# Part of the source-row look-ups of a graph attention stage moved from GpSimd gathers to TensorE one-hot products

## The reference, cut to what matters

```python
h = (x_flat @ W_gat).reshape(M, HEADS, NUM_EXPERTS)          # M = 32768 nodes, 4 heads x 4 values
a_src = (h * att_src).sum(-1);  a_dst = (h * att_dst).sum(-1)
e = leaky_relu(a_src[src] + a_dst[dst], negative_slope=0.2)   # one value per edge and head
e_max = segment_max(e, dst);  ee = exp(e - e_max[dst])
denom = segment_sum(ee, dst); alpha = ee / (denom[dst] + 1e-16)
agg = segment_sum(h[src] * alpha[:, :, None], dst) + b_gat    # 16 values per node
...                                                           # top 2 of 4 gates per node
for ei in range(NUM_EXPERTS):
    hh = gelu(x @ W1[ei] + b1[ei]);  out = out + g[..., None] * (hh @ W2[ei] + b2[ei])
```

## Time and profile before

| | us |
|---|---|
| median of three runs | 10518.87 |
| profiled execution, its own time | 10541.24 |
| span of that execution | 10539.5 |
| `edge_states`, its first DMA issue to the end of its last scan | 4594.0 to 9925.8 |
| busy in the span: GpSimd / TensorE / Vector / Scalar | 5766.4 / 4945.6 / 4253.4 / 2154.3 |

### The profile page before, as it was taken

One profiled execution on the slowest core, in us unless ns is written; L12 is line 12 of the kernel. 1 busy time (PEld: TensorE's weight loads), 2 busy tenths in 40 slices (PEclk: granted clock), 3 DMA queues, 4 the chain that ended last, 5 costly groups with the idle time before them and its releaser, 6 DMA issues. The chain is left out here.

```text
span 10539.5 us, 77438 instructions
## 1 busy us (share of the span) xinstructions
PE 4945.6 (47%) x21339; PEld 2904.5 (28%) x21339; DVE 4253.4 (40%) x9137; ACT 2154.3 (20%) x4043; POOL 5766.4 (55%) x5263
## 2 busy tenths in 40 slices
PE   6888888689936888821112111122111122111145
PEld 5556555567722444410000000000000000000011
DVE  5665665556679878711111111111111111111178
ACT  3434344333311222211111111111111111111000
POOL 2333333300032455367777777777777777777662
PEclk9888898899968999965556555556555556555577
DMA  2000000021110222131111111111111111111455
GB/s 89 34 34 26 26 25 24 38 77 57 57 58 30 54 55 52 34 71 33 34 36 36 38 33 34 33 37 39 33 34 33 34 36 39 34 33 34 59 183 187
DMA packets 388197, 510.48 MB, mean 48 GB/s; under 512 B 216517, under 2 KB 303358, under 8 KB 365442
## 3 DMA queue, kind: packets, MB, share of 16 engines
q1 hardware_dynamic: 191618, 258.32, 8.6%
q0 software_dynamic: 163968, 75.75, 6.3%
q10 hardware_dynamic: 32256, 171.98, 4.1%
HBM read 245.58 MB, written 263.86 MB: 48 GB/s over the span
## 5 line engine op out<-in xcount | busy, mean ns | idle before, releaser
L1663 POOL DMA_INDIRECT e_row<-rows_dram,e_idx x4096 | 4058.6, 991 | 1263.2 <-issue 1247.2
L1609 PE MATMUL e_bank<-e_hid,e_w 128*128 128x512 f32 x1024 | 591.7, 713 | 4217.1 <-ACT e_hid L1639 4217.1
L1696 DVE COPY e_idx<-e_allidx 128x64 int32 x64 | 13.8, 215 | 4374.0 <-DMA e_row<-rows_dram,e_idx 4374.0
L1609 PEld LDWEIGHTS e_bank<-e_hid,e_w 128*128 128x128 f32 x1024 | 220.7, 223 | 4520.3 <-issue 4520.3
L1647 ACT ACTIVATE e_ex<-e_dx 128x512 f32<-128x512 f32 x64 | 40.3, 630 | 3605.3 <-DVEq L1709 3605.3
L387 POOL COPY a_xc<-a_xp 128x1573 f32<-128x1573 f32 x104 | 405.9, 3907 | 678.1 <-PE a_bank L441 563.7
L1047 POOL DMA_INDIRECT c_yt<-yb_dram,keep_slots x256 | 383.0, 1496 | 587.0 <-DVE c_yg L1267 507.7
L396 POOL DMA_INDIRECT xb_dram<-a_so,a_sidx x256 | 251.6, 983 | 739.7 <-DVE a_sidx L669 490.5
L1602 PE MATMUL e_bank<-e_h,e_w 128*128 128x512 f32 x1024 | 508.4, 626 | 77.6 <-DMA e_h<-hn_dram 77.6
L199 DVE TENSOR_TENSOR a_cnta_hot<-a_cnta_iota,a_cnta_part 128x512 bf16<-128x512 bf16 x1184 | 519.9, 439 | 0.0
L1168 PE MATMUL c_conv<-c_xp,c_w 128*128 128x512 f32 x1152 | 513.7, 600 | 0.0
(11 more groups left out here) (352 smaller groups left out, 10083.1 us busy)
## 6 DMA issues: line engine op xcount, KB each, us to landing
e_row<-rows_dram,e_idx POOLq DMA_INDIRECT x4096
ys_dram<-e_y ACTq DMA_DIRECT2D x64, 1024.0 KB, 3.9
f_ye<-ys_dram SPq DMA_DIRECT2D x64, 1024.0 KB, 4.8
res_dram<-e_st ACTq DMA_DIRECT2D x64, 768.0 KB, 3.3
xb_dram<-a_taps SPq DMA_DIRECT2D x4, 5120.0 KB, 31.1
b_tok<-xb_dram SPq DMA_DIRECT2D x80, 256.0 KB, 2.7
yb_dram<-b_y ACTq DMA_DIRECT2D x80, 256.0 KB, 2.0
x_dram<-a_xs SPq DMA_DIRECT2D x9, 2048.0 KB, 6.3
```

The lines of the kernel that those rows point to most:

```text
L1609: mm = nc.tensor.matmul(bank[UPB + n % DNB][:], w2[:, n % NE, f], hid[:, n % 2, f], start=(f == 0), stop=(f == NF1 - 1))
L1663: nc.gpsimd.indirect_dma_start(row[:, s, u], None, rows, bass.IndirectOffsetOnAxis(ap=idx[:, s, u:u + 1], axis=0)).then_inc(gath[s], 16)
```

## The change

- Of the 64 edges of a chunk and partition, GpSimd now gathers the rows of 50 (`UP`). The last 14 (`XG`) are looked up on chip.
- The node table is loaded once into SBUF as `table` by 8 DMAs of 4096 pieces of 64 bytes each: node = (s, g, l), with l (0 to 127) the partition, g (8) and s (32). Only the 16 values of `h` are in it.
- `code` holds the low 10 bits of the source index, `high` the upper 5. For look-up k TensorE spreads the 128 codes over all partitions (L1629, a product with the identity, into PSUM `spread`), Vector compares them with the 8 x 128 low numbers and so makes the one-hot weights `hot` (L1772, 1024 elements), TensorE multiplies them with the table in 8 products of 128x128 by 128x512 (L1642, into PSUM `found`), and Vector masks the 32 candidates by the upper bits (L1791, 512 elements) and sums them (L1796, 512 to 16). `found`, `hot` and `prod` have two buffers each. After 14 look-ups Vector works out `a_src` of these edges (L1799 to L1801).
- TensorE's list is now, for each chunk: look-ups 0 and 1, the expert step, look-ups 2 to 13. The one-hot weights of look-ups 0 and 1 of the next chunk are made in this one.
- Vector does the 14 look-ups of a chunk ahead of all its former work on it.
- Scalar runs one expert step before the loop, and then the step of chunk n + 1 ahead of the exponentials of chunk n.
- The exponentials go to PSUM (`ex`), those used as weights also to SBUF (`weight`) by a second activation. The banks left for the experts are two for `up` and two for `down`.
- The wait for the stored states at the end of each turn is now a wait of each chunk for its own buffer. Scalar clears the semaphores of the block `experts` in `partition_starts`.

The core of the diff (declarations and the passing of arguments are left out):

```diff
         @block.sync
         def _(sp):
-            sp.dma_start(allidx[:, 0:FE], srcs).then_inc(consts, 16)
+            sp.dma_start(allidx[:, 0:FE], srcs).then_inc(listed, 16)
+            for g in range(HG):
+                sp.dma_start(table[:, g], table_g[g][:, :, 0:HF]).then_inc(tabled, 16)
             for dst, src in ((w1[:], w["w1"].rearrange("e d f -> d e f")),
                              (w2[:], w["w2"].rearrange("e (f p) d -> p e f d", p=P)),
-                             (b1[:], w["b1"]), (b2[:], w["b2"])):
+                             (b1[:], w["b1"]), (b2[:], w["b2"]), (att[:], att_src.broadcast_to([P, HF]))):
                 sp.dma_start(dst, src).then_inc(consts, 16)
 
...
         @block.tensor
         def _(pe):
+
+            def spread_code(k):
+                s, j = divmod(k % (2 * XG), XG)
+                nc.tensor.matmul(spread[:], code[:, s, j:j + 1].broadcast_to([P, P]), ident[:], start=True,
+                                 stop=True).then_inc(code_spread, 1)
+
             pe.wait_ge(consts, 80)
+            pe.wait_ge(coded, 1)
+            spread_code(0)
+            pe.wait_ge(tabled, 16 * HG)
             with pe.Fori(0, TURNS) as i:
+                def look_up(k):
+                    pe.wait_ge(hot_ready, 2 * XG * i + (k + 1))
+                    spread_code(k + 1)
+                    pe.wait_ge(masked, 2 * XG * i + (k + 1))
+                    for g in range(HG):
+                        mm = nc.tensor.matmul(found[k % 2][:].rearrange("p s c -> p (s c)"), hot[:, k % 2, g],
+                                              table[:, g].rearrange("p s c -> p (s c)"), start=(g == 0),
+                                              stop=(g == HG - 1))
+                    mm.then_inc(found_psum, 1)
+
...
-                up(0)
-                for n in range(TURN):
-                    if n + 1 < TURN:
-                        up(n + 1)
-                    down(n)
+                for s in range(2):
+                    for j in range(2):
+                        look_up(XG * s + j)
+                    up(STEP * s)
+                    for n in range(STEP * s, STEP * (s + 1)):
+                        if n + 1 < STEP * (s + 1):
+                            up(n + 1)
+                        down(n)
+                    for j in range(2, XG):
+                        look_up(XG * s + j)
+            pe.wait_ge(hot_ready, XG * CHUNKS + 1)
+            spread_code(1)
 
...
+            def states_of(i, s):
+                act.wait_ge(dx_ready, 2 * i + s + 1)
+                nc.scalar.activation(ex[:], dx[:], ACT.Exp)
+                nc.scalar.activation(weight[:], dx[:, 1], ACT.Exp).then_inc(ex_ready, 1)
+                act.wait_ge(st_ready, 2 * i + s + 1)
+                act.dma_start(res_c[2 * i + s], st[:, s]).then_inc(stored[s], 16)
+
+            experts_of(0, 0)
+            with act.Fori(0, TURNS - 1) as i:
+                experts_of(i, 1)
+                states_of(i, 0)
+                experts_of(i + 1, 0)
+                states_of(i, 1)
+            experts_of(TURNS - 1, 1)
...
+            def one_hot(k, first):
+                dve.wait_ge(code_spread, first + (k + 1))
+                nc.vector.tensor_tensor(hot[:, k % 2], spread[:].unsqueeze(1).broadcast_to([P, HG, P]),
+                                        lows[:].unsqueeze(2).broadcast_to([P, HG, P]), ALU.is_equal
+                                        ).then_inc(hot_ready, 1)
+
+            for k in range(2):
+                one_hot(k, 0)
+            K = 18
             with dve.Fori(0, TURNS) as i:
                 for s in range(2):
                     n = 2 * i + s
                     link = Chain(dve, chain, K * n)
+                    link(nc.vector.tensor_copy(code[:, 1 - s], codei[:, 0, bass.ds(n + 1, 1)].rearrange(
+                        "p n u -> p (n u)")))
+                    link(nc.vector.tensor_copy(high[:], codei[:, 1, bass.ds(n, 1)].rearrange("p n u -> p (n u)")))
+                    link(nc.vector.tensor_tensor(pick[:], highs[:].unsqueeze(1).broadcast_to([P, XG, HS]),
+                                                 high[:].unsqueeze(2).broadcast_to([P, XG, HS]), ALU.is_equal))
+                    for j in range(XG):
+                        k = XG * s + j
+                        dve.wait_ge(found_psum, 2 * XG * i + (k + 1))
+                        nc.vector.tensor_tensor(prod[:, k % 2], found[k % 2][:],
+                                                pick[:, j].unsqueeze(2).broadcast_to([P, HS, HF]), ALU.mult
+                                                ).then_inc(masked, 1)
+                        one_hot(k + 2, 2 * XG * i)
+                        dve.wait_ge(masked, 2 * XG * i + (k + 3))
+                        nc.vector.tensor_reduce(row[:, s, UP + j, 0:HF], prod[:, k % 2].rearrange("p s c -> p c s"),
+                                                AX.X, ALU.add).then_inc(picked, 1)
+                    dve.wait_ge(picked, 2 * XG * i + XG * (s + 1))
+                    link(nc.vector.tensor_tensor(aprod[:], row[:, s, UP:, 0:HF],
+                                                 att[:].unsqueeze(1).broadcast_to([P, XG, HF]), ALU.mult))
+                    link(nc.vector.tensor_reduce(row[:, s, UP:, HF:],
+                                                 aprod[:].rearrange("p u (h e) -> p u h e", e=NE), AX.X, ALU.add))
...
-                    dve.wait_ge(gath[s], 16 * U * i + 16 * U)
-
-                    nc.vector.tensor_copy(idx[:, s], allidx[:, bass.ds((2 * i + s + 2) * U, U)]
+                    dve.wait_ge(gath[s], 16 * UP * i + 16 * UP)
+
+                    nc.vector.tensor_copy(idx[:, s], allidx[:, bass.ds((2 * i + s + 2) * U, UP)]
                                           ).then_inc(idx_ready, 1)
...
+                    dve.wait_ge(stored[s], 16 * i + 16)
...
-                        add = msg[:, :, c // NE, c % NE] if c < HF else ex[:, 1, :, h]
+                        add = msg[:, :, c // NE, c % NE] if c < HF else weight[:, :, h]
-                for s in range(2):
-                    dve.wait_ge(stored[s], 16 * i + 16)
```

More of the change, by code:

```diff
@@ L1487, in _ @@
             sp.wait_ge(fixed, 16)
+        @block.scalar
+        def _(act):
+            for handle in ended:
+                act.sem_clear(handle)
         @block.gpsimd
@@ L1513, with edge_states @@
 K1 = NT // P
[L1516 to L1519 removed]
+def edge_states(nc, passed, rows, srcs, cont, v, res, hn, ys, ident, att_src, w):
+    U, XG = 64, 14
+    UP = U - XG
     TURNS = FE // (2 * U)
[L1521 removed]
+    CHUNKS = 2 * TURNS
+    UPB, DNB = 2, 2
+    HG, HS = 8, NHI // 8
     with ExitStack() as ctx:
@@ L1524, in edge_states @@
         sem = lambda n: ctx.enter_context(nc.semaphore(f"e_{n}"))
+        ps = lambda n, s: ctx.enter_context(nc.psum_tensor(f"e_{n}", s, F32))
         allidx = sb("allidx", [P, FE + 2 * U], I32)
-        idx = sb("idx", [P, 2, U], I32)
+        idx = sb("idx", [P, 2, UP], I32)
+        codei = sb("codei", [P, 2, CHUNKS + 1, XG], I32)
+        code = sb("code", [P, 2, XG])
+        high = sb("high", [P, XG])
+        lowi, lows = sb("lowi", [P, HG], I32), sb("lows", [P, HG])
+        highi, highs = sb("highi", [P, HS], I32), sb("highs", [P, HS])
+        table = sb("table", [P, HG, HS, HF])
+        att = sb("att", [P, HF])
+        hot = sb("hot", [P, 2, HG, P])
+        pick = sb("pick", [P, XG, HS])
+        prod = sb("prod", [P, 2, HS, HF])
+        aprod = sb("aprod", [P, XG, HF])
         same = sb("same", [P, 2, U])
@@ L1545, in edge_states @@
         b2 = sb("b2", [P, NE])
-        bank = [ctx.enter_context(nc.psum_tensor(f"e_bank{i}", [P, NT], F32)) for i in range(8)]
-        consts = sem("consts")
+        ex = ps("ex", [P, 2, U, NH])
+        spread = ps("spread", [P, P])
+        found = [ps(f"found{z}", [P, HS, HF]) for z in range(2)]
+        bank = [ps(f"bank{i}", [P, NT]) for i in range(UPB + DNB)]
+        consts, listed, tabled, made = sem("consts"), sem("listed"), sem("tabled"), sem("made")
         h_loaded = [sem(f"h_loaded{s}") for s in range(2)]
@@ L1632, in outputs @@
                                          bias=b2[:, e:e + 1]).then_inc(y_ready, 1)
-                for s in range(2):
[L1635 to L1649, removed]
+                for n in range(s * STEP, (s + 1) * STEP):
+                    for f in range(NF1):
+                        m = NF1 * n + f
+                        act.wait_ge(up_psum, NF1 * TURN * i + (m + 1))
+                        nc.scalar.activation(hid[:, n % 2, f], bank[m % UPB][:], ACT.Gelu,
+                                             bias=b1[:, n % NE, f:f + 1]).then_inc(up_ready, 1)
+                    if n % STEP:
+                        outputs(n - 1)
@@ L1650, in _ @@
+            experts_of(0, 0)
[5 more added lines that the diff above has]
+            experts_of(TURNS - 1, 1)
             for s in range(2):
-                act.wait_ge(stored[s], 16 * TURNS)
+                states_of(TURNS - 1, s)
```

(4 more changed lines are left out.)

51 lines of the change are left out of this document (37 added, 14 removed).

## The result

The changed kernel takes 13,549.67 us (median of four runs, 13,544.11 to 13,555.02), the kernel before 10,520.16. The ratio is 1.288, with a 95% interval of 1.286 to 1.291. The forecast was 9950 us with a range of 9770 to 10,300. The time moved the other way: the kernel got slower.

What follows compares the result with a forecast made beforehand. GpSimd's gathers bound the kernel before; with the change TensorE was to pace the look-ups. Rounds of 73.5 us gave a stage end of 9348 instead of 9925.8, 578 us less: forecast 9950 us, range 9770 to 10,300.

Steps and rivals of the forecast that it cites:

- One look-up: TensorE's table products and codes: 8 x 0.43 + 0.11 = 3.55 us; Vector needs 3.1 us, so TensorE sets the pace.
- The rule that was thrown out: True FP32 takes four TensorE passes: 0.85 us a product, 6.9 us a look-up; the sum used the trace row instead.
- the expert step: After look-ups 0 and 1: 16 TensorE products in 6.9 us, 12 Scalar activations; 8.0 us taken, bounds 6.9 and 9.8.
- The round as a sum: From the end of look-up 13 to the same point next chunk: 28.3 + 42.6 + 2.2, with hand-offs 73.5 us.
- the restart at the low clock: TensorE after its long idle time: some 4.4 us at half speed cost 2.2 us a round, bounds 0 and 4.
- Vector's terms: Vector's mask 0.69, comparison 1.22, sum 1.06 us (bounds 0.69 and 2.1); 20 scans 5.0 us as before.
- Start: TensorE starts at about 4640 us instead of 4606.2, behind the table load, judged by `f_tr`'s 39.0 us.
- "Slower": Rival, chance 0.10: TensorE stays at 1.2 GHz in the look-ups; round about 125 us, total near 13,200.
- its turning point: Where the change becomes slower: 9 us more a round, or 4.3 us a look-up from whatever cause.
- "GpSimd stays the bound": Rival, chance 0.05: the gathers still set the time, 64 x 63.4 us, total 9290; needs a round under 65.
- "Vector paces": Rival, chance 0.10: Vector's sum takes 2.1 us, so Vector needs 4.1 a look-up; round 78, total about 10,240.

Runs made afterwards that it cites:

- the experiment with two parts: The changed kernel with the node table split into two bf16 parts whose products add up in PSUM; 10,503.57 us, ratio 0.997 to the kernel before.
- the kernel with one part: The changed kernel with the node table rounded to bf16 and one-hot weights in bf16; 9412.74 us, ratio 0.893 to the kernel before.

## Why the prediction was wrong

**The failed step is "One look-up".** It took the distance of two TensorE instructions in the trace (0.43 us) for the time of an f32 product. An f32 product is two instructions. The prediction's rows held the proof: 64 expert steps with 8 `down` products are 512 products, and the line says x1024; the convolution has 9 taps, and its run is x18; the 4 products of 128 columns with the identity come as x8. Measured: 7.09 us a look-up instead of 3.55. Over 14 look-ups 49.6 us of a round, 3170 us in all. This one factor of two turns 578 us of gain into a loss.

**The rule that was thrown out held.** The Trainium skill, "FP8 and Floating Point Precision", section "TensorE Precision Notes", has true FP32 take four passes; from it the prediction worked out 0.85 us a product and 6.9 us a look-up, and then set it aside for the row. The trace agrees with the rule: two instructions of 0.429 are 0.858 us, four times the 0.216 of a bf16 product in the experiment with two parts. It shows two instructions to a product; how many passes are in each it does not show. Row and rule differed by exactly two, and that should have sent the reader to the counts. The mistake was the reading of the row, not the row.

**The same mistake in the expert step.** The prediction had 16 products in 6.9 us and a step of 8.0, with bounds of 6.9 and 9.8. Measured 14.1 us. Two of its rows spoke against it: Scalar is still in the middle of one step from 6028.9 to 6042.9, 14 us, and TensorE, idle for 66 of 83 us by the prediction's own division, was busy for the other 17 with these 16 products, part of it at the low clock. The step adds 6.1 us a round, 390 in all, so it and the look-ups are 3560 of the 3600 us between forecast and result. It also says why the kernel with the pace of 3.67 us a look-up lands at 10,504: its round is 81.7, where the prediction's sum had 73.5, and of the difference of 8.2 the expert step is 6.1, the look-ups 1.7.

**The round as a sum was right.** With 0.86 us a product the same list gives 14.2 + 13.8 (16 products) + 13.2 (exponentials, `msg` and scans, head and first weights) + 85.1 + 2.2 = 128.5 us against 129.4 measured. The step is 0.3 us over its 16 products, where 1.1 had been put for the two banks fewer. Its order held too: `msg` waited for Scalar (22.2 us instead of 8, as the two look-ups and the step before it were twice as long), TensorE for the weights of look-up 2 (13.9 us, forecast 13), the restart at the low clock cost 2.3 (2.2), GpSimd fell idle.

**Vector's terms.** The mask took 0.69 and the comparison 1.21 us, as taken. The sum with the far inner step took 1.00, within its bounds and near the 1.06 chosen. Scans with one input in PSUM cost nothing more: 4.00 for 16, before 4.02.

**Start.** TensorE began at 4629.0 instead of the forecast 4640, as the table's DMAs took 33 us (4591.1 to 4623.9) and not the 39 of `f_tr`.

**The rivals.** "Slower" gave 13,200 us, near the measured 13,550, but its cause is refuted: the granted clock is 1.00 over the look-ups. It comes near by luck, as half the clock and twice the instructions both double the price of a product. What decided was its turning point, stated as 9 us more a round or 4.3 us a look-up from whatever cause. "GpSimd stays the bound" needed a round under 65 us, and that exists: with two bf16 parts, 12 look-ups and the exponentials moved. "Vector paces" came true in the kernel with one part. What the prediction cited of the Trainium skill, "SBUF — State Buffer", section "Who interferes with whom" (there: a Vector instruction with two SBUF inputs contends with a GpSimd instruction that reads SBUF), was borne out by the experiment with the exponentials in PSUM: 3.55 us gathers back to 0.94, 174 us by the medians and 166 expected; the change carries this gain too, but GpSimd is idle there and it buys nothing.

## What to carry to other kernels

Before a duration from a trace becomes a price, divide the count of its instructions by the count in the program: a product in f32 has two lines here, one in bf16 one. When a rule of the Trainium skill and a row differ by a whole factor, ask first whether the row was read in another unit; here it was. And a split of work between engines has a balance that follows from two prices, here 7.1 us a look-up on TensorE, on top of 30 us for the rest of its round (129.4 - 14 x 7.1), against 1.25 a gather on GpSimd. At 14 look-ups the new engine was the bound by 67 us a chunk (129.4 against 50 x 1.25); at 6 both were level (73 against 72.5, measured 71.9).

## What the runs showed of the hardware

- An f32 product with a one-hot operand is dearer than the same product in three bf16 parts: 8 x 3 products in 5.18 us of a look-up (5.40 with the codes) against 6.87 (7.09). Three parts of 8 bits hold the 24 bits of an f32 value. Two parts take 3.45.
- Weight loads of 128x128 (0.19 us in f32, 0.10 in bf16) run beside the products, which start 0.43 (f32 instruction) and 0.216 us (bf16) apart with new weights for each. They are not what spaces them in f32: with new weights for each too, instructions of 128 columns start 0.11 us apart. No run leaves the loads out.
- A run of 20 scans with two SBUF inputs holds up one gather of GpSimd for 2.6 us; with one of the inputs in PSUM the longest gather of 4096 took 1.02 us. Splitting the table, in the kernel with two parts, shows it a second time. A gather issued within the subtraction of two SBUF tensors ended only behind that and the copy to bf16 after it, 5.79 us instead of 0.94:

```profile
4630.38 4.42 DVE L1776 TENSOR_TENSOR e_table<-e_table,e_part 128x4096 f32<-128x4096 f32 x1
4631.46 5.79 POOL L1743 DMA_INDIRECT e_row<-rows_dram,e_idx  x1 [0.30 <-issue]
4634.84 2.29 DVE L1778 CAST e_part<-e_table 128x4096 bf16<-128x4096 f32 x1
```
